# Linear expert layer: shares transposed and bias products formed inside their own batch, in PSUM banks of their own, the bias added once per two token tiles, and the next batch's chain started earlier

## The chip, the cores and the metric

One Trainium2 chip, one core. The metric is device time in microseconds (us) of one execution of the whole program. The program computes two layers of a small model, in four phases that run one after the other, each in a block of its own. The change is in the last phase only.

## The reference, cut to what matters

The last phase computes this, on 8 batches of 512 tokens with 256 channels, all in 32-bit floats (`x` is first normalised over its channels, and the output is added to the un-normalised `x`):

```python
scores = jnp.maximum(x @ gate_W + gate_b, 1e-4)          # 8 experts
p = jax.nn.softmax(scores, axis=-1)
_, topk_idx = jax.lax.top_k(p, 2)
topk_mask = jax.nn.one_hot(topk_idx, 8).sum(-2) > 0
w = jnp.maximum(p, 0.1)
w = w / take_along_axis(w, topk_idx, axis=-1).sum(-1, keepdims=True)
comb = jnp.where(topk_mask, w, 0)                         # the shares
y = jnp.einsum('bsd,edf->bsef', x, expert_W) + expert_b
out = jnp.einsum('bsef,bse->bsf', y, comb) / 2
```

Every token goes through all 8 experts, and the shares weigh the 8 results. The bias part is `comb @ expert_b`, a product with only 8 rows to sum over, and needs the shares transposed.

## The kernel before, in words

`moe_linear_phase` (from L1312) is written out by hand for five engine queues that meet only in semaphores. A batch is 512 tokens, in four token tiles `k` of 128. Experts are taken in pairs `e`; a unit `u` from 0 to 15 is one tile with one pair (k = u // 4, e = u % 4). For each unit TensorE (L1656) makes six matmuls of 128x512 into one of four banks of `o_ps`: 32-bit precision is built from an upper and a lower part of activations and weights. Odd units are weighted and taken out by ScalarE (`weigh_odd`, L1468) and summed by GpSimd (`add_odd`, L1403); even units are weighted and added into `x` by VectorE (`accumulate`, two instructions at L1570). At a tile's last unit GpSimd adds the odd sum to `x` (L1407). Unit u must wait on TensorE until the unit four earlier has been taken out of its bank.

Beside the units, each batch has a chain for the next one. It starts with the mean and variance on VectorE (`variance`, L1014 and L1019), a root on ScalarE (`root`, L1425 and L1427), the rest of the normalisation on VectorE (`normalise`, five small instructions L1024 to L1028 and four of 128x256 at L1030, which make `xn`), eight transposes on TensorE (`turn_rows`, L1612) and two copies on ScalarE (`take_rows`, L1436 and L1437). GpSimd forms the lower part (`low`, L1385), TensorE the gate product (`gate`, 16 small matmuls, L1620), VectorE the scores and the top two (`scores`, `first_choice`, `second_choice`, `shares`, L1519 to L1553), with an exponential on ScalarE (`exponents`, L1442). Then come the transposes of the shares on TensorE (`turn_comb`, L1627), a copy on ScalarE (`take_comb`, L1449), and the bias product (`biases`, L1634), which VectorE adds to two tiles of `x` in one instruction (L1564).

The order on each queue is fixed by the unit numbers. In batch n before the change:

- TensorE: bias product before units 0 and 8; `turn_rows(n+1)` after unit 3, `gate(n+1)` after 6, `turn_comb(n+1)` after 14. The gate product, the row transposes and the share transposes all use `f_ps`.
- VectorE: bias added ahead of units 0 and 8; `normalise(n+1)` after unit 0, `scores(n+1)` after 6, `first_choice` after 8, `second_choice` after 10, `shares` after 12, `variance(n+2)` after 14.
- ScalarE: `take_rows(n+1)` after unit 3, `exponents(n+1)` after 7, `take_comb(n+1)` after 14, `root(n+2)` after 15.
- GpSimd: `low(n+1)` after unit 7, and at start-up the lower weight parts of pairs 2 and 3 (L1393) only after the first batch's shares.
- SyncE stores a batch once its four tiles are done and loads the one three further on.

Before the first unit, TensorE does `turn_rows(0)`, `gate(0)`, `turn_comb(0)`, and then waits for the copied shares.

Of the kernel before, what the change touches and what calls it, by code (L numbers as in the profile page):

```python
# [7 lines left out]
ALU = mybir.AluOpType  # L8
# [5 lines left out]
P = 128  # L14
# [1297 lines left out]
def moe_linear_phase(nc, sem, A, layer, x_in, x_out):  # L1312
# [5 lines left out]
    with ExitStack() as ctx:  # L1318
# [22 lines left out]
        b_ps = ctx.enter_context(nc.psum_tensor("m1_b_ps", [P, 2, 2 * D], F32))  # L1341
# [8 lines left out]
        with nc.Block() as block:  # L1350
# [26 lines left out]
            def _(pool):  # L1377
# [10 lines left out]
                for e in range(PAIRS):  # L1388
                    if e == 2:
                        low(0)  # L1390
                        pool.wait_ge(S["comb_ready"], 1)
                    pool.wait_ge(S["w_hi"], e + 1)
                    pool.tensor_tensor(w_lo[:, e, :, :], raw[:, e, :, :], w_hi[:, e, :, :], ALU.subtract).then_inc(S["w_ready"], 1)  # L1393

                def add_odd(n, u):
# [8 lines left out]
                    if e == PAIRS - 1:  # L1404
                        pool.wait_ge(S["odd_added"], q + 1)
                        pool.wait_ge(S["acc_done"], UNITS // 2 * n + 2 * (k + 1))
                        pool.tensor_tensor(x[:, n % XB, k, :], x[:, n % XB, k, :], odd[:, k, :], ALU.add).then_inc(S["tile_done"], 1)  # L1407

                for n in range(NB):
                    for u in range(UNITS):  # L1410
                        if u % 2:
                            add_odd(n, u)
                        if u == 7 and n + 1 < NB:
                            low(n + 1)

            @block.scalar
            def _(act):
# [26 lines left out]
                def take_comb(n):  # L1444

                    act.wait_ge(S["combT_ps"], n + 1)
                    if n > 1:
                        act.wait_ge(S["b_ready"], 2 * (n - 1))
                    act.activation(combT[:, n % 2, :], f_ps[0:E, 0, :], ACT.Copy).then_inc(S["combT_ready"], 1)  # L1449
# [22 lines left out]
                upper(0)  # L1472
                upper(1)
# [3 lines left out]
                upper(2)  # L1477
                upper(3)
                take_comb(0)
                for n in range(NB):  # L1480
                    act.wait_ge(S["comb_ready"], n + 1)
                    for u in range(UNITS):
                        if u % 2:
                            weigh_odd(n, u)
                        if n + 1 < NB:
                            if u == 3:
                                take_rows(n + 1)
                            if u == 7:
                                exponents(n + 1)
                            if u == 14:  # L1490
                                take_comb(n + 1)
                        if u == 15 and n + 2 < NB:
                            root(n + 2)

            @block.vector
            def _(dve):
# [59 lines left out]
                def accumulate(n, u):  # L1556
# [5 lines left out]
                    if u % PAIRS == 0 and k % 2 == 0:  # L1562
                        dve.wait_ge(S["b_ready"], 2 * n + k // 2 + 1)
                        dve.tensor_tensor(x[:, n % XB, k:k + 2, :], b_ps[:, k // 2, :].rearrange("p (a c) -> p a c", a=2), x[:, n % XB, k:k + 2, :],  # L1564
                                          ALU.add).then_inc(S["b_added"], 1)
                        dve.wait_ge(S["b_added"], 2 * n + k // 2 + 1)
                    else:
                        dve.wait_ge(S["acc_done"], q)
# [7 lines left out]

                variance(0)
                normalise(0)
                variance(1)
                scores(0)  # L1580
# [3 lines left out]
                for n in range(NB):  # L1584
                    dve.wait_ge(S["comb_ready"], n + 1)
                    for u in range(0, UNITS, 2):
                        accumulate(n, u)
                        if n + 1 < NB:
                            if u == 0:
                                normalise(n + 1)  # L1590
                            if u == 6:
                                scores(n + 1)
                            if u == 8:
                                first_choice(n + 1)
                            if u == 10:
                                second_choice(n + 1)
                            if u == 12:
                                shares(n + 1)
                        if u == 14 and n + 2 < NB:
                            variance(n + 2)  # L1600

            @block.tensor
            def _(pe):
                pe.wait_ge(S["const_in"], 80)

                def turn_rows(n):

                    pe.wait_ge(S["xn_ready"], n + 1)
                    wait(pe, S["combT_ready"], n)
# [13 lines left out]
                def turn_comb(n):  # L1623

                    pe.wait_ge(S["comb_ready"], n + 1)
                    for k in range(4):
                        last = pe.transpose(f_ps[0:E, 0, k * P:(k + 1) * P], comb[:, n % 2, k, :], ident[:, :])  # L1627
                    last.then_inc(S["combT_ps"], 1)

                def biases(n, k):  # L1630

                    wait(pe, S["b_added"], 2 * n + k // 2 - 1)
                    for a in range(2):
                        last = pe.matmul(b_ps[:, k // 2, a * D:(a + 1) * D], combT[:, n % 2, (k + a) * P:(k + a + 1) * P], eb[:, :], start=True, stop=True)  # L1634
# [4 lines left out]
                turn_comb(0)  # L1639
                for n in range(NB):  # L1640
                    pe.wait_ge(S["xT_lo_ready"], n + 1)
                    pe.wait_ge(S["combT_ready"], n + 1)
                    for u in range(UNITS):
                        k, e = u // PAIRS, u % PAIRS
                        tok = slice(k * P, (k + 1) * P)
                        if u % PAIRS == 0 and k % 2 == 0:
                            biases(n, k)
# [10 lines left out]
                        if n + 1 < NB:  # L1658
                            if u == 3:
                                turn_rows(n + 1)  # L1660
                            if u == 6:
                                gate(n + 1)
                            if u == 14:
                                turn_comb(n + 1)
# [475 lines left out]
```

## Time and profile before

| | us |
|---|---|
| median of 3 runs | 2230.68 (2228.68 to 2231.84) |
| the profiled execution's own time | 2226.19 |
| its span, first to last instruction | 2224.4 |
| the last phase in that span, from about 1951.8 to the end | about 272.6 |

The other three phases fill the first 1951 us and their instructions are not touched. In the views, times are us from the start of the span. A timeline row is start, duration, engine, line, operation, output and inputs, shapes and how many instructions are merged; brackets at its end hold the engine's idle time before it and what ended that. "x2" with a duration of 1.60 is two instructions from the start of the first to the end of the second. PE is TensorE's matmuls, PEld its weight loads, DVE VectorE, ACT ScalarE, POOL GpSimd, SPq the queue of SyncE. Matmuls are pipelined, so that spacing between starts, not duration, is what one costs.

### The profile page before, as it was taken

What the parts mean: (1) busy time and instruction counts of PE and PEld (TensorE: products, weight loads), DVE (VectorE), ACT (ScalarE), POOL (GpSimd) and SP (SyncE); (2) the same over time, 40 slices, a digit from 0 to 9 for tenths busy, and PEclk for the clock granted to TensorE, in tenths of its full rate; (3) what the DMA queues carried; (4) which work ended last, traced back from release to release, by engine and by line L of the source; (5) the groups of instructions that cost most, each with busy time, mean ns of one, the idle gap of its engine ahead of it and who ended that gap; (6) DMA issues with size and microseconds to landing.
All of it is one profiled execution on the core that took longest, in us unless ns stands there. A gap on an engine that the chain in (4) does not pass through costs nothing. (4 is left out here: it accounts for less than half of the span.)

```text
span 2224.4 us, 32244 instructions
## 1 busy us (share of the span) xinstructions
PE 1909.3 (86%) x9910; PEld 1116.9 (50%) x9910; DVE 1656.6 (74%) x2326; ACT 1241.3 (56%) x2642; POOL 1427.7 (64%) x1164
## 2 busy tenths in 40 slices
PE   2499999999973999975799999999999998759998
PEld 1244444444422899972345454545454433347776
DVE  4477788787744646530799999999999999836664
ACT  1066666676662433325787777777778675323332
POOL 7334444543334344430899999999999999834444
PEclk9599999999875999987999999999999999969999
DMA  3554545544234454430413131222213130021100
GB/s 80 108 103 96 110 107 116 113 99 122 69 123 149 84 88 76 75 51 19 162 42 130 58 114 75 97 91 81 106 66 121 42 132 30 0 78 39 38 26 22
DMA packets 231224, 185.68 MB, mean 83 GB/s; under 512 B 148729, under 2 KB 201601, under 8 KB 231058
## 3 DMA queue, kind: packets, MB, share of 16 engines
q1 hardware_dynamic: 216178, 162.61, 25.9%
q0 software_dynamic: 13296, 17.77, 4.6%
q10 hardware_dynamic: 1584, 3.24, 0.5%
q8 instruction: 85, 1.39, 0.3%
q14 instruction: 81, 0.66, 0.1%
HBM read 134.07 MB, written 49.49 MB: 83 GB/s over the span
## 5 line engine op out<-in xcount | busy, mean ns | idle before, releaser
L1817 POOL TENSOR_TENSOR mb_dbu<-mb_dtu,mb_bbc 128x1024 f32<-128x1024 f32 x256 | 598.6, 2360 | 5.2 <-DVE mb_da_ps L1974 2.4
L473 ACT ACTIVATE ex_plain<-at_t_ps 128x512 f32<-128x512 f32 x512 | 289.5, 595 | 178.9 <-PE at_t_ps L851 176.8
L1974 DVE TENSOR_TENSOR_SCAN mb_da_ps<-mb_da_ps,mb_dbu 128x1024 f32<-128x1024 f32 x160 | 365.3, 2283 | 4.0 <-ACT mb_da_ps L1867 3.3
L2009 PE MATMUL mb_y_ps<-mb_hc,lw_ident 128*128 128x512 f32 x640 | 311.7, 610 | 43.1 <-DVE mb_hc L1981 42.7
L610 DVE TENSOR_REDUCE at_mx<-at_s_ps 128x2 f32<-128x1024 f32 x256 | 310.9, 1219 | 47.7 <-PE at_s_ps L860 46.2
L860 PE MATMUL at_s_ps<-ex_w 48*128 48x512 f32 x512 | 226.4, 504 | 37.4 <-DVE at_mx L610 24.2
L851 PE MATMUL at_t_ps<-ex_w 64*128 64x512 f32 x512 | 220.0, 487 | 11.6 <-ACT ex_plain L473 6.4
L1823 POOL TENSOR_TENSOR mb_hp<-mb_hp,mb_cbc 128x1024 f32<-128x1024 f32 x96 | 226.1, 2356 | 0.0
L1201 POOL DMA_INDIRECT x<-m_o,m_xs x71 | 113.7, 1602 | 173.3 <-DMA x<-m_o,m_xs 106.6
L1972 DVE TENSOR_TENSOR_SCAN mb_hp<-mb_da_ps,mb_dbu 128x1024 f32<-128x1024 f32 x96 | 218.9, 2280 | 6.4 <-POOL mb_dbu L1817 5.4
L2009 PEld LDWEIGHTS mb_y_ps<-mb_hc,lw_ident 128*128 128x128 f32 x640 | 118.2, 192 | 201.8 <-issue 126.5
L1981 DVE TENSOR_TENSOR mb_hc<-mb_da_ps,mb_cbc 128x1024 f32<-128x1024 f32 x160 | 195.4, 1221 | 12.6
L2009 PE MATMUL mb_y_ps<-mb_hp,lw_ident 128*128 128x512 f32 x384 | 184.2, 602 | 14.7 <-POOL mb_hp L1823 14.7
L851 PEld LDWEIGHTS at_t_ps<-ex_w 64*128 64x128 f32 x512 | 86.9, 194 | 173.3 <-ACT ex_plain L473 132.6
L1866 ACT ACTIVATE mb_da_ps<-mb_dt,lw_a_neg 128x512 f32<-128x512 f32 x256 | 172.6, 674 | 0.0
L1867 ACT ACTIVATE mb_da_ps<-mb_dt,lw_a_neg 128x511 f32<-128x511 f32 x256 | 171.9, 671 | 0.0
L1865 ACT ACTIVATE mb_da_ps<-mb_zero 128x1 f32<-128x1 f32 x256 | 43.0, 168 | 215.9 <-DVE mb_hc L1981 174.2
L1290 PE MATMUL m_y_ps<-ex_w,m_xsT_hi 128*128 x568 | 157.2, 337 | 0.1
L1403 POOL TENSOR_TENSOR m_odd<-m_odd,m_odd_in 128x256 f32<-128x256 f32 x96 | 70.6, 735 | 123.8 <-ACT m_odd_in L1468 118.6
L871 PE MATMUL at_o_ps<-ex_plain 128*32 128x512 f32 x1024 | 146.0, 644 | 0.1
L422 POOL CAST at_qk_hi<-at_qk 128x512 fp32r<-128x512 f32 x32 | 19.6, 612 | 179.8 <-DVE at_qk L754 179.8
L2009 PEld LDWEIGHTS mb_y_ps<-mb_hp,lw_ident 128*128 128x128 f32 x384 | 73.0, 192 | 104.6 <-issue 75.8
(322 smaller groups left out, 4117.8 us busy)
## 6 DMA issues: line engine op xcount, KB each, us to landing
mb_bbc<-mb_scr SPq DMA_DIRECT2D x64, 512.0 KB, 6.0
mb_cbc<-mb_scr SPq DMA_DIRECT2D x64, 512.0 KB, 5.7
ex_w<-at_scr SPq DMA_DIRECT2D x384, 64.0 KB, 2.3
m_xs<-rt_rows SPq DMA_DIRECT2D x71, 129.0 KB, 2.1
at_scr<-at_qk_hi SPq DMA_DIRECT2D x32, 256.0 KB
at_scr<-at_qk_lo SPq DMA_DIRECT2D x32, 256.0 KB
at_xin<-in_x SPq DMA_DIRECT2D x32, 128.0 KB, 2.3
ex_plain<-in_x SPq DMA_DIRECT2D x8, 512.0 KB
```

Of the source, the lines that this page charges most:

```text
L473: act.activation(probs[:, c, h, :], t_ps[:, k % 2, :], ACT.Exp, scale=SCALE).then_inc(exp_done, 1)
L610: dve.tensor_reduce(out, s_ps[:, m % 2, :, :], AX.X, ALU.max).then_inc(max_done, 1)
L851: pe.matmul(t_ps[:, k % 2, :], of_head(kst, r, h, 64, c), of_head(qst, r, h, 64), start=True, stop=True).then_inc(t_ready, 1)
L860: last = pe.matmul(s_ps[:, m % 2, a, :], of_head(qst, u % 4, h + 2 * a, 48, c), of_head(kst, u % 4, h + 2 * a, 48), start=True, stop=True)
L1817: pool.tensor_tensor(dbu[:, q % 3, :, :], dtu_2, bbc[:, 2 * p:2 * p + 2, :], ALU.mult).then_inc(S["dbu_ready"], 1)
L1823: pool.tensor_tensor(hp[:, r, :, :], hp[:, r, :, :], cbc[:, 2 * p:2 * p + 2, :], ALU.mult).then_inc(S["hp_ready"], 1)
L1866: act.activation(da_ps[:, q % 2, 0, :], dt[:, d % 2, :], ACT.Exp, scale=a_neg[:, d, 2 * p:2 * p + 1])
L1867: act.activation(da_ps[:, q % 2, 1, 1:T], dt[:, d % 2, 1:T], ACT.Exp, scale=a_neg[:, d, 2 * p + 1:2 * p + 2]).then_inc(S["da_ready"], 1)
L1972: dve.tensor_tensor_scan(hp[:, t % 3, :, :].rearrange("p j t -> p (j t)"), da, add, 0.0, ALU.mult, ALU.add).then_inc(S["scan_done"], 1)
L1974: dve.tensor_tensor_scan(da, da, add, 0.0, ALU.mult, ALU.add).then_inc(S["scan_done"], 1)
L1981: dve.tensor_tensor(hc[:, t % 2, :, :], da_ps[:, r, :, :], cbc[:, 2 * p:2 * p + 2, :], ALU.mult).then_inc(S["hc_ready"], 1)
L2009: last = pe.matmul(y_ps[:, v % 2, :], ident[:, :], src[:, j, :], start=False, stop=(q == tile_last[v] and j == 1))
```

## The change

The shares of a batch are now transposed, copied and multiplied with the biases inside that batch. They get a bank of their own (`c_ps`); the bias product has one bank where it had two, and is added after units 6 and 14 (by `add_biases`), no longer ahead of units 0 and 8. GpSimd's additions at the end of a tile become `finish`, two in a row after units 7 and 15, behind a wait for the added bias. The chain moves up. On TensorE `turn_rows(n+1)` follows unit 0, and `turn_comb(n)` with `gate(n+1)` follows unit 3. On VectorE `scores` follows unit 4, the choices units 6 and 8, `shares` and `variance(n+2)` unit 10, and `normalise(n+2)` comes after unit 14 of batch n. At start-up TensorE goes from `gate(0)` straight to the units, ScalarE splits all four weight pairs ahead of `take_rows(0)`, VectorE normalises batch 1 ahead of `scores(0)`, and GpSimd drops its wait for the shares.

```diff
-        b_ps = ctx.enter_context(nc.psum_tensor("m1_b_ps", [P, 2, 2 * D], F32))
+        b_ps = ctx.enter_context(nc.psum_tensor("m1_b_ps", [P, 2 * D], F32))
+        c_ps = ctx.enter_context(nc.psum_tensor("m1_c_ps", [P, T], F32))
@@ gpsimd
                     if e == 2:
                         low(0)
-                        pool.wait_ge(S["comb_ready"], 1)
...
-                    if e == PAIRS - 1:
-                        pool.wait_ge(S["odd_added"], q + 1)
-                        pool.wait_ge(S["acc_done"], UNITS // 2 * n + 2 * (k + 1))
-                        pool.tensor_tensor(x[:, n % XB, k, :], x[:, n % XB, k, :], odd[:, k, :], ALU.add).then_inc(S["tile_done"], 1)
+                def finish(n, k):
+                    pool.wait_ge(S["odd_added"], 4 * (PAIRS - 1) * n + (PAIRS - 1) * (k + 1))
+                    pool.wait_ge(S["b_added"], 2 * n + k // 2 + 1)
+                    pool.tensor_tensor(x[:, n % XB, k, :], x[:, n % XB, k, :], odd[:, k, :], ALU.add).then_inc(S["tile_done"], 1)
                 for n in range(NB):
-                    for u in range(UNITS):
-                        if u % 2:
-                            add_odd(n, u)
-                        if u == 7 and n + 1 < NB:
+                    for u in range(1, UNITS, 2):
+                        add_odd(n, u)
+                        if u == 5 and n + 1 < NB:
                             low(n + 1)
+                        if u in (7, 15):
+                            finish(n, u // PAIRS - 1)
+                            finish(n, u // PAIRS)
@@ scalar
                 root(0)
-                upper(0)
-                upper(1)
+                for e in range(PAIRS):
+                    upper(e)
                 take_rows(0)
                 root(1)
                 exponents(0)
-                upper(2)
-                upper(3)
-                take_comb(0)
                 for n in range(NB):
-                    act.wait_ge(S["comb_ready"], n + 1)
                     for u in range(UNITS):
+                        if u == 1:
+                            act.wait_ge(S["comb_ready"], n + 1)
                         if u % 2:
                             weigh_odd(n, u)
+                        if u == 3:
+                            take_comb(n)
                         if n + 1 < NB:
-                            if u == 3:
+                            if u == 0:
                                 take_rows(n + 1)
-                            if u == 7:
+                            if u == 5:
                                 exponents(n + 1)
-                            if u == 14:
-                                take_comb(n + 1)
-                        if u == 15 and n + 2 < NB:
+                        if u == 11 and n + 2 < NB:
                             root(n + 2)
@@ vector
-                    if u % PAIRS == 0 and k % 2 == 0:
-                        dve.wait_ge(S["b_ready"], 2 * n + k // 2 + 1)
-                        dve.tensor_tensor(x[:, n % XB, k:k + 2, :], b_ps[:, k // 2, :]..., ALU.add).then_inc(S["b_added"], 1)
-                        dve.wait_ge(S["b_added"], 2 * n + k // 2 + 1)
-                    else:
-                        dve.wait_ge(S["acc_done"], q)
+                    wait(dve, S["acc_done"], q)
...
+                def add_biases(n, k):
+                    dve.wait_ge(S["b_ready"], 2 * n + k // 2 + 1)
+                    dve.wait_ge(S["acc_done"], UNITS // 2 * n + 2 * (k + 2))
+                    rows = x[:, n % XB, k:k + 2, :]
+                    dve.tensor_tensor(rows, b_ps[:, :].rearrange("p (a c) -> p a c", a=2), rows, ALU.add).then_inc(S["b_added"], 1)
                 variance(1)
+                normalise(1)
                 scores(0)
...
                         accumulate(n, u)
+                        if u in (6, 14):
+                            add_biases(n, u // PAIRS - 1)
                         if n + 1 < NB:
-                            if u == 0:
-                                normalise(n + 1)
+                            if u == 4:
+                                scores(n + 1)
                             if u == 6:
-                                scores(n + 1)
+                                first_choice(n + 1)
                             if u == 8:
-                                first_choice(n + 1)
+                                second_choice(n + 1)
                             if u == 10:
-                                second_choice(n + 1)
-                            if u == 12:
                                 shares(n + 1)
-                        if u == 14 and n + 2 < NB:
-                            variance(n + 2)
+                        if n + 2 < NB:
+                            if u == 10:
+                                variance(n + 2)
+                            if u == 14:
+                                normalise(n + 2)
@@ tensor
                 def turn_rows(n):
                     pe.wait_ge(S["xn_ready"], n + 1)
-                    wait(pe, S["combT_ready"], n)
+                    wait(pe, S["z_ready"], n)
...
                 def biases(n, k):
-                    wait(pe, S["b_added"], 2 * n + k // 2 - 1)
+                    pe.wait_ge(S["combT_ready"], n + 1)
+                    wait(pe, S["b_added"], 2 * n + k // 2)
...
                 gate(0)
-                turn_comb(0)
                 for n in range(NB):
                     pe.wait_ge(S["xT_lo_ready"], n + 1)
-                    pe.wait_ge(S["combT_ready"], n + 1)
                     for u in range(UNITS):
-                        if u % PAIRS == 0 and k % 2 == 0:
-                            biases(n, k)
...
-                        if n + 1 < NB:
-                            if u == 3:
-                                turn_rows(n + 1)
-                            if u == 6:
+                        if u == 0 and n + 1 < NB:
+                            turn_rows(n + 1)
+                        if u == 3:
+                            turn_comb(n)
+                            if n + 1 < NB:
                                 gate(n + 1)
-                            if u == 14:
-                                turn_comb(n + 1)
+                        if u in (5, 12):
+                            biases(n, 0 if u == 5 else 2)
```

## Rows read from the trace of the kernel before

**Rows 1.** Busy time by stretch: the columns, and one stretch of 30 us.

```profile
core 0: us, PE busy (x) PEld busy (x) DVE busy (x) ACT busy (x) POOL busy (x), PEclk, DMA share, GB/s
2050.00:2080.00 30.00, 28.21 (x135) 22.04 (x134) 19.12 (x60) 9.74 (x22) 14.14 (x17) 1.00 0.12 36
```

**Rows 2.** Waits, last phase: who waited for whom, total us, times, longest.

```profile
PE m_f_ps L1612 <- DVE m_xn L1030: 18.7, 7, 15.8
PE m_f_ps L1627 <- DVE m_comb L1553: 15.4, 8, 5.7
```

**Rows 3.** Chain that ended last, one batch: start, us, engine, tile and line.

```profile
2051.47 1.09 PE m_f_ps L1612 x8
2052.56 4.14 PE m_o_ps L1656 x18
2056.70 1.68 PE m_f_ps L1620 x16
2059.89 1.05 PE m_b_ps L1634 x4
...
2072.07 0.60 PE m_f_ps L1627 x4
...
2081.31 1.09 PE m_f_ps L1612 x8
```

**Rows 4.** TensorE's timeline: last matmuls before its two halts in one batch.

```profile
2050.59 0.40 PE L1656 MATMUL m_o_ps<-m_w_lo,m_xT_hi 128*128 128x512 f32 x1
...
2070.37 0.40 PE L1656 MATMUL m_o_ps<-m_w_lo,m_xT_hi 128*128 128x512 f32 x1
```

**Rows 5.** VectorE's timeline around a batch's start, bias to `xn`.

```profile
2046.96 0.69 DVE L1564 TENSOR_TENSOR m_x<-m_b_ps,m_x 128x512 f32<-128x512 f32 x1 [2.04 <-PE m_o_ps L1656]
2047.69 1.00 DVE L1570 SCALAR_TENSOR_TENSOR m_x<-m_o_ps,m_comb,m_x 128x256 f32<-128x256 f32 x2
2048.61 0.15 DVE L1024 TENSOR_TENSOR m_rs<-m_rs 128x4 f32<-128x4 f32 x1
...
2049.40 0.60 DVE L1028 TENSOR_TENSOR m_rs<-m_rs 128x4 f32<-128x4 f32 x1
2050.04 1.38 DVE L1030 TENSOR_SCALAR m_xn<-m_x,m_mv,m_rs 128x256 f32<-128x256 f32 x4
```

**Rows 6.** GpSimd's timeline around the same batch's start.

```profile
2044.81 1.60 POOL L1403 TENSOR_TENSOR m_odd<-m_odd,m_odd_in 128x256 f32<-128x256 f32 x2 [3.58 <-ACT m_odd_in L1468]
2046.49 0.73 POOL L1407 TENSOR_TENSOR m_x<-m_x,m_odd 128x256 f32<-128x256 f32 x1
2049.24 0.74 POOL L1403 TENSOR_TENSOR m_odd<-m_odd,m_odd_in 128x256 f32<-128x256 f32 x1 [2.02 <-ACT m_odd_in L1468]
```

**Rows 7.** Timeline at start-up: GpSimd beside VectorE's four `xn` instructions.

```profile
1960.47 4.69 POOL L1393 TENSOR_TENSOR m_w_lo<-m_raw,m_w_hi 128x1024 fp32r<-128x1024 f32 x2 [8.61 <-ACT m_w_hi L1454]
1960.48 5.48 DVE L1030 TENSOR_SCALAR m_xn<-m_x,m_mv,m_rs 128x256 f32<-128x256 f32 x4
```

**Rows 8.** Timeline of the start-up, from the first gate product on.

```profile
1970.08 3.58 PE L1620 MATMUL m_f_ps<-m_gw,m_xT 128*128 128x8 f32 x16 [2.03 <-ACT m_xT_hi L1437]
1970.17 2.35 POOL L1385 TENSOR_TENSOR m_xT_lo<-m_xT,m_xT_hi 128x1024 fp32r<-128x1024 f32 x1 [5.01 <-ACT m_xT_hi L1437]
1970.24 0.20 ACT L1427 ACTIVATE m_rs<-m_rs 128x4 f32<-128x4 f32 x1
1979.31 1.02 PE L1627 MATMUL m_f_ps<-m_ident,m_comb 128*8 128x128 f32 x4 [5.65 <-DVE m_comb L1553]
1983.07 0.80 PE L1656 MATMUL m_o_ps<-m_w_hi,m_xT_hi 128*128 128x512 f32 x1
...
2014.34 1.13 PE L1634 MATMUL m_b_ps<-m_eb,m_combT 8*128 8x256 f32 x4
```

**Rows 9.** Busy time by stretch at start-up, columns as in the first group.

```profile
1986.00:1989.00 3.00, 3.00 (x8) 2.32 (x8) 2.67 (x9) 0.35 (x1) 0.00 (x0) 0.50 0.00 0
1989.00:1992.00 3.00, 3.00 (x16) 2.45 (x16) 2.41 (x6) 0.80 (x3) 0.81 (x1) 0.97 0.00 0
```

**Rows 10.** TensorE's timeline in the third phase, after idle times of 2.36 and 3.35 us.

```profile
1881.73 1.99 PE L2009 MATMUL mb_y_ps<-mb_hc,lw_ident 128*128 128x512 f32 x4 [2.36 <-DVE mb_hc L1981]
1921.27 3.47 PE L2009 MATMUL mb_y_ps<-mb_hc,lw_ident 128*128 128x512 f32 x4 [3.35 <-DVE mb_hc L1981]
```

**Rows 11.** Timeline of the end of the span.

```profile
2217.70 0.40 PE L1656 MATMUL m_o_ps<-m_w_lo,m_xT_hi 128*128 128x512 f32 x1
...
2220.34 0.72 POOL L1407 TENSOR_TENSOR m_x<-m_x,m_odd 128x256 f32<-128x256 f32 x1
2221.09 0.37 SPq L1370 DMA_DIRECT2D x<-m_x  x1
```

More of the change, by code:

```diff
@@ L1448, in take_comb @@
                         act.wait_ge(S["b_ready"], 2 * (n - 1))
-                    act.activation(combT[:, n % 2, :], f_ps[0:E, 0, :], ACT.Copy).then_inc(S["combT_ready"], 1)
+                    act.activation(combT[:, n % 2, :], c_ps[0:E, :], ACT.Copy).then_inc(S["combT_ready"], 1)
                 def upper(e):
@@ L1561, in accumulate @@
                     dve.wait_ge(S["o_ready"], UNITS * n + u + 1)
-                    if u % PAIRS == 0 and k % 2 == 0:
-                        dve.wait_ge(S["b_ready"], 2 * n + k // 2 + 1)
-                        dve.tensor_tensor(x[:, n % XB, k:k + 2, :], b_ps[:, k // 2, :].rearrange("p (a c) -> p a c", a=2), x[:, n % XB, k:k + 2, :],
-                                          ALU.add).then_inc(S["b_added"], 1)
-                        dve.wait_ge(S["b_added"], 2 * n + k // 2 + 1)
-                    else:
-                        dve.wait_ge(S["acc_done"], q)
+                    wait(dve, S["acc_done"], q)
                     for a in range(2):
@@ L1625, in turn_comb @@
                     pe.wait_ge(S["comb_ready"], n + 1)
+                    wait(pe, S["combT_ready"], n)
                     for k in range(4):
-                        last = pe.transpose(f_ps[0:E, 0, k * P:(k + 1) * P], comb[:, n % 2, k, :], ident[:, :])
+                        last = pe.transpose(c_ps[0:E, k * P:(k + 1) * P], comb[:, n % 2, k, :], ident[:, :])
                     last.then_inc(S["combT_ps"], 1)
                 def biases(n, k):
-                    wait(pe, S["b_added"], 2 * n + k // 2 - 1)
+                    pe.wait_ge(S["combT_ready"], n + 1)
+                    wait(pe, S["b_added"], 2 * n + k // 2)
                     for a in range(2):
-                        last = pe.matmul(b_ps[:, k // 2, a * D:(a + 1) * D], combT[:, n % 2, (k + a) * P:(k + a + 1) * P], eb[:, :], start=True, stop=True)
+                        last = pe.matmul(b_ps[:, a * D:(a + 1) * D], combT[:, n % 2, (k + a) * P:(k + a + 1) * P], eb[:, :], start=True, stop=True)
                     last.then_inc(S["b_ready"], 1)
```

## The prediction

> **What bounds the kernel now.** I read four views, in this order. The busy time by stretch [rows 1] says that the last phase is TensorE's: 28.21 of 30 us busy at full clock, VectorE 19.12, GpSimd 14.14, ScalarE 9.74. So only what makes TensorE wait or work can move the end. The waits [rows 2] name the two halts: the row transposes wait for `xn`, the share transposes for `comb`. The chain [rows 3] gives the period: from one batch's row transposes at 2051.47 to the next at 2081.31 is 29.84 us, and nearly every piece is TensorE's. Last, TensorE's timeline [rows 4] gives the size of the halts. Eighteen matmuls take 4.14 us [rows 3], so 0.23 each and a unit of six 1.37. The last matmul before the row transposes starts at 2050.59, so these could have begun at 2050.82; they began at 2051.47, a halt of 0.65. Likewise 2070.37 + 0.23 = 2070.60 against 2072.07, a halt of 1.47. The period adds up: 96 matmuls 21.9, row transposes 0.9, gate 1.8, two bias products 2.5, share transposes 0.5, halts 2.1. All that a better order can win per batch is the 2.1, and at the start-up the 5.65 us that TensorE is idle for the first shares [rows 8].
>
> **The share halt goes.** `turn_comb(n)` follows unit 3 of its own batch, long after the shares. Its copy by ScalarE (0.6 us) has units 4 and 5 (2.7 us) to hide under before the bias product. I cost these moves at 0, and the work itself stays: same transposes, products and additions, so 27.6 us per batch without halts (0.1 less than before, as gate and share transposes are adjacent). If the cover were gone, the bias product would wait 0.6.
>
> **The row halt grows: the main term.** `turn_rows(n+1)` now follows unit 0, while VectorE makes its `xn` only after unit 14 of the batch before and after a bias addition. Between the two TensorE has units 15 and 0 alone, 2.74 us. VectorE needs, from the rows of the same instructions [rows 5]: 0.2 until it sees unit 14 (as before its bias addition at 2046.96; unit 0 ended at about 2046.8), 1.03 for the two accumulations, 0.6 for the bias addition, 5 x 0.2 for the small instructions (2048.61 to 2049.40 is four of them), 1.38 for L1030, 0.05 to TensorE. That is 4.26, so the halt is at least 4.26 - 2.74 = 1.5 us however free the rest is.
>
> To that comes GpSimd. The fifth small instruction takes 0.60 us where its like takes 0.15, and it ends (2050.00) just as a GpSimd addition (2049.24 + 0.74) ends [rows 5, 6]. At start-up four `xn` instructions take 5.48 us instead of 1.38; beside them lie two GpSimd instructions of 4.69 in all [rows 7]. The first instruction ended with the first of these, the second with the second, and the last two were free. So a running GpSimd instruction holds such a VectorE instruction to its end, and one gets through per GpSimd instruction. The accumulations and the bias addition, which read PSUM, show no such loss [rows 5].
>
> The Trainium skill's page "SBUF — State Buffer", section "Who interferes with whom", speaks against the change here: it tells of a lock on a shared port pair, taken for a whole instruction, by every tensor-tensor operation with both inputs in SBUF and by tensor-scalar operations. By that rule all nine instructions can be held; if only L1028 and L1030 could, where rows show it, the halt below would be 2.8 and the sum 3.6 less. Up to those two lines the trace agrees.
>
> Where do the two meet? GpSimd's last two additions of the batch start 0.74 us after unit 15 (2044.81 against 2044.07, 0.23 after its last matmul started) and span 1.60, then 0.08 and 0.73 for the tile's end [rows 6]. The change puts a second tile's end behind that: busy from +0.74 to about +3.9. VectorE's small instructions begin at +0.46. Two pass; the third (L1026, of the same operation and shape as the fifth) is held to +1.5, the fifth to +2.4, the first `xn` instruction to +3.2, the second to +4.1; the last two take 0.66. TensorE starts the transposes at +4.8 instead of +1.37: a halt of 3.4. Bounds: 1.5 (no holding) to 4.0 (VectorE also late into unit 14). I take 3.4, as its rows are the same engines and lines. VectorE's stretch from unit 6 on (bias, both choices, shares, variance, four accumulations) comes out at 24.95 after the row transposes, against 25.0 for the end of unit 14: just in time, with no slack; hence the upper bound. `root(n+2)` after unit 11 keeps ScalarE waiting for the variance, and unit 13's weighing behind it, by 0.9 us; its bank is needed two units later, so 0.
>
> From the start of batch 1 to the end of the last unit is 2014.24 to 2217.93 = 203.7 before [rows 8, 11]. After: six batches with a halt, 6 x (27.6 + 3.4) = 186.0, and a last one without row transposes and gate, 24.9: 210.9. **+7.2.**
>
> **Start-up.** The units can follow the gate at 1973.8 instead of 1983.07 [rows 8]. Unit 0 ends at 1976.4, at the lower clock (0.43 us a matmul). Then `turn_rows(1)` waits for the second `xn` and for `z_ready`, that is `scores(0)`, queued behind `normalise(1)`. That starts at 1970.5 [rows 8] and meets three GpSimd instructions without a gap, since the wait for the shares is gone: `low(0)` to 1972.5 and two weight parts of 2.35 to 1977.2. Held once by each, it ends at about 1979.0, the scores at 1979.8. Row transposes 1.8, units 1 to 3 at the lower clock 7.7, share transposes and gate 2.6: unit 4 starts at 1991.9. Then 12 units 16.5 and two bias products 2.5: batch 1 starts at 2010.9 against 2014.24. **-3.3** (from 0, if the raised clock comes later, to -6, if it comes sooner; before, it came at 1989.2, after 6 us of units [rows 8, 9]). Splitting all weights before `take_rows(0)` hides under ScalarE's idle time up to 1968.1: 0, or +2 if weight data landed late.
>
> **End.** Both tiles' ends now stand behind the last unit, one more instruction of 0.72 before the store [rows 11]: **+0.7**. The bias addition ends earlier than GpSimd's odd sums, so its wait is free.
>
> **Clock.** TensorE now pauses 3.4 us in each of six batches, with only transposes behind it. In the third phase a pause of 3.35 was followed by four matmuls in 3.47 us, one of 2.36 by four in 1.99 [rows 10]: the granted clock, 2.4 GHz before, was at its lower level, 1.2 GHz, after the one and not after the other. A longer pause is thus more likely than not to cost about 1.6 (3.47 against 1.88 to 1.99). I take 4.5 times in six, midway between half and all: **+7.2**, with 0 and 6 x 2 = 12 as ends.
>
> **Sum.** 7.2 - 3.3 + 0.7 + 7.2 = +11.8. The profiled execution took 2226.19 (span 2224.4 plus 1.8 around it), 4.5 below the median of the runs shown; the difference is put on the median: 2230.7 + 11.8 = 2242.5.
>
> **The rivals.**
> 1. The halt is as I say, but the clock holds: +4.6, 2235.3. For it: TensorE's halts of 1.3 us left the clock at 1.00 [rows 1]. Against: [rows 10].
> 2. Faster: GpSimd and VectorE hardly meet, because ScalarE or GpSimd is out of step there. The halt is 1.5, short enough for the clock: 6 x (27.6 + 1.5) + 24.9 = 199.5, so -4.2 - 3.3 + 0.7 = -6.8, 2223.9. It decides below a halt of 2.6, with the clock held, where 6 x 2.6 is the 15.8 that the rest wins (rival 4). Against: GpSimd's four additions follow unit 15 by semaphores, and cannot be earlier or later by much.
> 3. VectorE becomes the bound from unit 6 on and starts its bias addition some 1.5 us late: halt 5 us, 6 x 1.6 more and the clock lost every time (+2.4): 2254. For it: the walk above leaves that stretch no slack. Against: 1.5 us is as much as all the holding that I counted at the batch's start.
> 4. The change does what it says in full, no halt is left: 6 x 27.6 + 24.9 = 190.5, with start-up and end -15.8, 2214.9. Against: the 1.5 us above needs no contention.
>
> **Chances.** Forecast 0.51, rival 1 0.2, rival 2 0.14, rival 3 0.11, rival 4 0.04. A measurement of this kernel tells about 0.2% (4.5 us) from no change. Rival 2 and 4 are faster, less a part of rival 2 near the line: 0.15. Rival 1 straddles the upper line: with half of it and the rest of rival 2 the same has 0.15. Slower 0.70. The range leaves out rival 4 and the outer parts of rivals 2 and 3: 2226 to 2252.
>
> **What would show it.** Right: the waits list has one large TensorE entry, row transposes for L1030, six times 3 us or more, none for `comb`; L1030 and the small instructions before it stretch beside GpSimd's; the period is 31 to 33 us; the clock by stretch falls below 1.00 in units 1 to 3. Wrong: L1030 at 1.38 for four and a period below 29.8, or the first unit not at about 1974. The weakest steps are how many pauses cost the clock, and where exactly GpSimd's additions fall.

## The result, and the profile after

The changed kernel is slower: median 2249.57 us of 6 runs (2243.15 to 2252.72) against 2229.94 of 6 runs of the kernel before; ratio 1.0089, 95% interval 1.0073 to 1.0105, some 19.6 us. The forecast was 2242.5 in a range of 2226 to 2252. The profiled execution took 2250.02, its span 2248.2. Its last phase, from the ScalarE table load at its head to the span's end, takes 291.98 us (from 1956.22) against 272.64 before (from 1951.76). That is 19.3 more, so all of the difference lies there.

Busy time of the whole span, after:

```profile
PE 1930.6 (86%) x9910; PEld 1131.0 (50%) x9910; DVE 1673.1 (74%) x2326; ACT 1240.6 (55%) x2642; POOL 1426.2 (63%) x1164
```

TensorE has the same 9910 matmuls and is busy some 21 us longer (1909.3 before). Waits (columns as in [rows 2]), and the chain of one batch (as in [rows 3]):

```profile
PE m_f_ps L1619 <- DVE m_xn L1030: 37.9, 7, 15.9
PE m_f_ps L1619 <- DVE m_p L1524: 3.5, 1, 3.5
```

```profile
2119.04 1.97 PE m_f_ps L1619 x8
2121.01 5.87 PE m_o_ps L1661 x18
2127.32 1.69 PE m_f_ps L1627 x16
2131.87 1.05 PE m_b_ps L1643 x4
...
2153.17 1.97 PE m_f_ps L1619 x8
```

The wait for `comb` is gone. The wait for `xn` went from 18.7 [rows 2] to 37.9, and without the first wait of 15.9 it is six of 3.67. The period is 34.13 where it was 29.84. Two pieces have grown though their instructions are the same: the eight row transposes, 1.97 where [rows 3] has 1.09, and the eighteen matmuls behind them, 5.87 where it has 4.14. That is the clock, as the busy time by stretch says (columns as in [rows 1]):

```profile
2110.00:2140.00 30.00, 26.34 (x117) 21.20 (x116) 16.86 (x46) 8.78 (x20) 12.14 (x15) 0.89 0.10 36
2119.00:2122.00 3.00, 2.96 (x11) 2.76 (x12) 0.86 (x2) 0.95 (x2) 0.00 (x0) 0.50 0.41 137
2122.00:2125.00 3.00, 3.00 (x9) 2.30 (x8) 0.00 (x0) 1.82 (x4) 0.43 (x1) 0.56 0.46 160
```

Here is the stretch that ends the pause:

```profile
2117.00:2119.50 2.50, 0.46 (x2) 0.46 (x3) 2.43 (x7) 0.00 (x0) 0.55 (x1) 0.66 0.39 137
```

Right behind the pause (2119 to 2122) the granted clock is 0.50, the lower of the two levels, 1.2 GHz, and the units of the next 5 us or so still run at it. Read in stretches of half a microsecond, the clock falls at about 2117.8, in the pause itself, and is back at about 2124.6: it is low for 6.8 us, 5.6 of them behind the start of the row transposes. The pauses before 2050.65, 2084.85, 2153.17 and 2187.30 look the same. The first one differs: the clock falls only at 2018.8, 1.25 us behind the start of the transposes at 2017.55, and is back at 2022.2, low for 3.4 us.

VectorE and GpSimd at the same halt; the columns are start, us, engine and line, and idle time before in brackets:

```profile
2112.10 2.08 DVE L1566 SCALAR_TENSOR_TENSOR m_x<-m_o_ps,m_comb,m_x 128x256 f32<-128x256 f32 x4
2114.29 0.69 DVE L1578 TENSOR_TENSOR m_x<-m_b_ps,m_x 128x512 f32<-128x512 f32 x1
2114.89 0.45 DVE L1024 TENSOR_TENSOR m_rs<-m_rs 128x4 f32<-128x4 f32 x1
2115.38 0.17 DVE L1025 TENSOR_SCALAR m_rs<-m_mv 128x4 f32<-128x4 f32 x1
2115.58 0.63 DVE L1026 TENSOR_TENSOR m_rs<-m_rs 128x4 f32<-128x4 f32 x1
2116.25 0.65 DVE L1027 TENSOR_SCALAR m_rs<-m_rs 128x4 f32<-128x4 f32 x1
2116.93 0.64 DVE L1028 TENSOR_TENSOR m_rs<-m_rs 128x4 f32<-128x4 f32 x1
2117.61 1.38 DVE L1030 TENSOR_SCALAR m_xn<-m_x,m_mv,m_rs 128x256 f32<-128x256 f32 x4
```

```profile
2113.56 0.74 POOL L1403 TENSOR_TENSOR m_odd<-m_odd,m_odd_in 128x256 f32<-128x256 f32 x1 [4.13 <-ACT m_odd_in L1472]
2114.59 1.60 POOL L1403 TENSOR_TENSOR m_odd<-m_odd,m_odd_in 128x256 f32<-128x256 f32 x2 [0.29 <-ACT m_odd_in L1472]
2116.15 1.40 POOL L1409 TENSOR_TENSOR m_x<-m_x,m_odd 128x256 f32<-128x256 f32 x2
2114.98 0.40 PE L1661 MATMUL m_o_ps<-m_w_lo,m_xT_hi 128*128 128x512 f32 x1
2119.04 1.97 PE L1619 MATMUL m_f_ps<-m_ident,m_xn 128*128 128x128 f32 x8 [3.66 <-DVE m_xn L1030]
```

GpSimd's five additions lie nearly without a gap from 2113.56 to 2117.55. Beside them four of VectorE's small instructions, which take 0.15 to 0.2 each when they are free, take 0.45, 0.63, 0.65 and 0.64; each ends just as a GpSimd addition ends. The last matmul of unit 0 starts at 2114.98, and by the 0.23 of the prediction the halt is 2119.04 - 2115.21 = 3.83. It is 3.82 to 3.83 in all six batches (the profile's own idle time reads 3.66 to 3.67).

### The profile page after: what moved, and what is told of

Read it like the earlier page. It is cut to its first block and busy times, and to the rows that moved or that the text cites. A ratio compares the mean times of both kernels' runs of the same rounds, so it can differ in the third digit from the quotient of the medians.

```text
span 2248.2 us, 32281 instructions
## 1 busy us (share of the span) xinstructions
PE 1930.6 (86%) x9910; PEld 1131.0 (50%) x9910; DVE 1673.1 (74%) x2326; ACT 1240.6 (55%) x2642; POOL 1426.2 (63%) x1164
## 5 line engine op out<-in xcount | busy, mean ns | idle before, releaser
L2015 PE MATMUL mb_y_ps<-mb_hc,lw_ident 128*128 128x512 f32 x640 | 316.3, 618 | 41.4 <-DVE mb_hc L1987 40.8
L422 POOL CAST at_qk_hi<-at_qk 128x512 fp32r<-128x512 f32 x32 | 19.5, 609 | 181.2 <-DVE at_qk L754 181.2
L1566 DVE SCALAR_TENSOR_TENSOR m_x<-m_o_ps,m_comb,m_x 128x256 f32<-128x256 f32 x128 | 61.7, 482 | 96.7 <-PE m_o_ps L1661 93.1
```

Of the source, the lines that this page charges most:

```text
L2015: last = pe.matmul(y_ps[:, v % 2, :], ident[:, :], src[:, j, :], start=False, stop=(q == tile_last[v] and j == 1))
```

## The experiments

All are edits of the changed kernel, whose line numbers they keep to within a few. What stands in the halt is in dispute (VectorE's fixed order alone, or GpSimd beside it), and so is what the pause costs through the clock. One table for all; "idle" is TensorE's idle time ahead of the row transposes, from batch 1 on; "low clock" is how many of those six pauses cost the clock; "period" is from one batch's transposes to the next's; these three and the last phase are read from the one profiled execution of each kernel; the kernel before ran beside them, median 2228.42 for the first four (31 runs) and 2228.56 for the last four (9 runs).

| kernel | median us (runs) | ratio to before, 95% | last phase | idle | low clock | period |
|---|---|---|---|---|---|---|
| after | 2249.57 (6) | 1.0089 (1.0073 to 1.0105) | 291.98 | 3.67 | 6 of 6 | 33.1, then 34.1 to 34.2 |
| e1_fill | 2234.84 (10) | 1.0029 (1.0017 to 1.0042) | 277.75 | 0.98 | 0 of 6 | 31.57 |
| e2_late_finish | 2228.08 (10) | 0.9999 (0.9987 to 1.0011) | 275.91 | 2.71 | 2 of 6 | 30.56; 33.44, 32.22 |
| e3_rows_late | 2223.45 (10) | 0.9987 (0.9973 to 1.0001) | 263.42 | 1.53 | 0 of 6 | 29.39 |
| e4_old_chain | 2220.23 (10) | 0.9966 (0.9952 to 0.998) | 263.83 | 1.08 | 0 of 6 | 28.95 |
| e5_bias_behind | 2208.6 (5) | 0.9912 (0.9899 to 0.9926) | 253.11 | 0 | 0 of 6 | 27.65 |
| e6_after_bias_behind | 2227.6 (1) | | 272.03 | 2.01 | 3 of 6 | 29.85; 31.47 |
| e7_all | 2205.89 (5) | 0.9902 (0.9889 to 0.9916) | 251.28 | 0 | 0 of 6 | 27.65, once 28.15 |
| e8_root_first | 2237.02 (1) | | 285.1 | 3.67 | 5 of 6 | 31.53, then 33.1 to 34.1 |

**Is it the pause that costs the clock?** The first kernel leaves VectorE's halt as it is, and fills it.

```diff
                 def turn_rows(n):
 
+                    if n > 1:
+                        pe.wait_ge(S["combT_ready"], n - 1)
+                        for _ in range(12):
+                            pe.matmul(c_ps[:, :], xT_hi[:, (n - 1) % 2, 0, 0:P], w_hi[:, 0, 0, :], start=True, stop=True)
                     pe.wait_ge(S["xn_ready"], n + 1)
```

> The changed kernel, with 12 extra matmuls of 128x512 (2.7 us at the full clock, result unused) put on TensorE ahead of the row transposes' wait, in batches 1 to 6, into the bank of the transposed shares. They fit into the halt of 3.8 us. Clock theory (the pause makes the clock fall, and that costs 1.6 to 2.6 us a batch beside the pause itself): the first transpose of a batch starts no later, the clock stays at 1.00, some 12 to 15 us off 2249.6: about 2236, still slower than before. Rival (the low clock after the halt has another cause, or costs nothing that the next halt would not take anyway): 2248 to 2251.

TensorE's timeline and one stretch of busy time:

```profile
2105.71 2.91 PE L1618 MATMUL m_c_ps<-m_w_hi,m_xT_hi 128*128 128x512 f32 x12
2109.59 1.09 PE L1623 MATMUL m_f_ps<-m_ident,m_xn 128*128 128x128 f32 x8 [0.98 <-DVE m_xn L1030]
```

```profile
2109.60:2112.60 3.00, 3.00 (x17) 2.62 (x18) 0.81 (x2) 1.87 (x3) 0.00 (x0) 1.00 0.49 132
```

The row transposes start 3.88 us behind unit 0, as late as after the change, and yet the clock is 1.00, they take 1.09, and the period is 31.57 against 34.13: 2.6 us a batch, for more work. The phase is 14.2 shorter and the median 14.7, of which up to 1.5 may lie between the two sets of runs: the kernel before had 2229.94 beside the changed kernel and 2228.42 here. The kernel is still 0.3% slower than the one before, as expected. So the pause costs twice, once as idle time and once in the clock. From the row transposes behind the first of the six pauses to the end of the last unit it takes 209.2 us (2014.87 to 2224.03), against 223.65 of the changed kernel (2017.55 to 2241.20): the clock is 14.5 us of the loss.

**Is GpSimd in the halt?** The two `finish` of a batch's last tiles go behind unit 1 of the next batch, away from VectorE's small instructions; VectorE's order stays.

```diff
-                        if u in (7, 15):
+                        if u == 1 and n:
+                            finish(n - 1, 2)
+                            finish(n - 1, 3)
+                        if u == 7 or u == 15 and n == NB - 1:
                             finish(n, u // PAIRS - 1)
```

> The changed kernel, with GpSimd's two tile ends behind unit 15 moved behind unit 1 of the next batch; TensorE's and VectorE's orders are untouched. Holding theory (a running GpSimd instruction holds a VectorE instruction to its end): L1027 and L1028 take 0.17 and not 0.65, so the halt shrinks by 0.9 to 1.0 from 3.8 to 2.9, 6 us in six batches; if the shorter pause saves some of the clock, up to 14 more: 2230 to 2244, 2242 if not. Rival (VectorE is late by its own load, GpSimd does not matter): halt 3.8, 2248 to 2251.

VectorE, GpSimd and TensorE at one halt:

```profile
2072.46 0.63 DVE L1026 TENSOR_TENSOR m_rs<-m_rs 128x4 f32<-128x4 f32 x1
2073.12 0.17 DVE L1027 TENSOR_SCALAR m_rs<-m_rs 128x4 f32<-128x4 f32 x1
2073.32 0.16 DVE L1028 TENSOR_TENSOR m_rs<-m_rs 128x4 f32<-128x4 f32 x1
2071.46 1.60 POOL L1403 TENSOR_TENSOR m_odd<-m_odd,m_odd_in 128x256 f32<-128x256 f32 x2 [0.27 <-ACT m_odd_in L1475]
2074.96 1.09 PE L1622 MATMUL m_f_ps<-m_ident,m_xn 128*128 128x128 f32 x8 [2.72 <-DVE m_xn L1030]
```

L1026 is held to the end of the odd additions, as before the edit. L1027 and L1028, whose neighbours were the two `finish`, fall from 0.65 and 0.64 to 0.17 and 0.16: 0.96 together, and the halt is 0.96 shorter. The period is 30.56 where the clock holds, which four pauses of six did. Six halts shorter by 0.96 are 5.8. The clock costs 2.9 and 1.7 in two pauses, 4.5 in all, where the changed kernel lost 14.5, so 10.0 more: together 15.8. The phase is 16.1 shorter. The ratio, 0.9999, can't be told from the kernel before. The median, 2228.08, is 2 below the expected 2230 to 2244, as most of the clock was kept.

**Does the place of the row transposes decide?** They go behind unit 2, with `take_rows` and `gate` as much later.

```diff
-                            if u == 0:
+                            if u == 1:
                                 take_rows(n + 1)
...
-                        if u == 0 and n + 1 < NB:
+                        if u == 2 and n + 1 < NB:
                             turn_rows(n + 1)
                         if u == 3:
                             turn_comb(n)
-                            if n + 1 < NB:
-                                gate(n + 1)
+                        if u == 4 and n + 1 < NB:
+                            gate(n + 1)
```

> The changed kernel, with the row transposes on TensorE behind unit 2 instead of unit 0 (the two copies on ScalarE behind unit 1's weighing, the gate product behind unit 4). VectorE's and GpSimd's orders are untouched. Theory (the halt is the gap between xn and the place where TensorE asks for it): two units of 1.37 more cover, halt 3.8 - 2.7 = 1.1, clock kept, 16 + 14 us off: about 2219, 11 faster than before. Rival (VectorE is the bound from unit 6 on and is late everywhere): TensorE waits elsewhere for the same time and the kernel stays above 2240.

The halt is 1.69 (idle 1.53) and not the 1.1 that two units of cover leave of 3.83. VectorE and GpSimd:

```profile
2072.92 1.93 DVE L1030 TENSOR_SCALAR m_xn<-m_x,m_mv,m_rs 128x256 f32<-128x256 f32 x4
2073.00 0.72 POOL L1403 TENSOR_TENSOR m_odd<-m_odd,m_odd_in 128x256 f32<-128x256 f32 x1
```

Units 1 and 2 now run ahead of the transposes, so unit 1's odd addition comes earlier and meets L1030: four in 1.93, not 1.38. The 0.55 is what was missing. Edits of TensorE's order move GpSimd's additions too. With no low clock left, the phase is 28.6 shorter. The median, 2223.45, misses the expected 2219, and its ratio, 0.9987 with an interval up to 1.0001, does not tell it from the kernel before. The rival (above 2240) is out.

**The shares moved alone.** Shares and bias as in the change, the rest of the chain where it was before.

```diff
-                            if u == 0:
+                            if u == 3:
                                 take_rows(n + 1)
...
+                            if u == 0:
+                                normalise(n + 1)
...
-                            if u == 14:
-                                normalise(n + 2)
...
-                        if u == 0 and n + 1 < NB:
-                            turn_rows(n + 1)
                         if u == 3:
                             turn_comb(n)
                             if n + 1 < NB:
-                                gate(n + 1)
+                                turn_rows(n + 1)
+                        if u == 6 and n + 1 < NB:
+                            gate(n + 1)
```

> One part alone: shares transposed and bias product formed in their own batch, own banks, bias added after units 6 and 14, units starting right after the first gate product, as in the changed kernel; but the chain for the next batch at its places of before (xn after unit 0, row transposes after unit 3, gate after 6, scores after 6, choices after 8 and 10, shares after 12, variance after 14). Theory (the moved chain alone made it slower): the share halts (7 x 1.5) and the 5.6 us at the start go, row halts stay near 0.7: 2213 to 2219, some 14 faster than before. Rival (the new order of bias and shares costs something itself): 2228 or more.

This half of the change is worth having: 0.9966, and the period falls from 29.82 to 28.95. That is less than the share halt of 1.47, since the row halt grew from 0.65 to about 1.2. The median, 2220.23, is 8 us below the kernel before and not the expected 14: the first row transposes also waited 3.96 us, with the clock low for 6.8 us around them. The rows of one later halt:

```profile
2076.80 0.74 DVE L1027 TENSOR_SCALAR m_rs<-m_rs 128x4 f32<-128x4 f32 x1
...
2077.77 1.83 DVE L1030 TENSOR_SCALAR m_xn<-m_x,m_mv,m_rs 128x256 f32<-128x256 f32 x4
...
2079.66 1.09 PE L1617 MATMUL m_f_ps<-m_ident,m_xn 128*128 128x128 f32 x8 [1.08 <-DVE m_xn L1030]
```

Again two GpSimd additions are met, one by L1027 and one by L1030.

**The bias addition out of the way.** On the third kernel's order, the batch's second bias addition goes behind `normalise(n+2)`. So `xn` no longer waits for it, and `finish`, which does wait for it, can't start beside the small instructions.

```diff
-                        if u in (6, 14):
+                        if u == 6 or u == 14 and n + 2 >= NB:
                             add_biases(n, u // PAIRS - 1)
...
                                 normalise(n + 2)
+                                add_biases(n, 2)
```

> As the kernel with the row transposes behind unit 2, and VectorE adds the second bias product behind the normalisation instead of ahead of it (batches 0 to 5). Theory (what stands on VectorE between unit 14 and xn, and what GpSimd does at that time, sets the halt): the bias addition's 0.6 leaves the path, and GpSimd's two tile ends, which wait for it, come later and hold nothing ahead of xn (0.9): the row halt falls from 1.7 to 0.2, period from 29.4 to 27.9, about 9 us off: 2214. Rival (VectorE's load from unit 6 on is the bound, order within it does not matter): halt 1.7, 2223.

```profile
2063.55 1.75 DVE L1030 TENSOR_SCALAR m_xn<-m_x,m_mv,m_rs 128x256 f32<-128x256 f32 x4
2065.21 0.68 DVE L1578 TENSOR_TENSOR m_x<-m_b_ps,m_x 128x512 f32<-128x512 f32 x1
2066.04 1.42 POOL L1409 TENSOR_TENSOR m_x<-m_x,m_odd 128x256 f32<-128x256 f32 x2 [1.87 <-DVE m_x L1578]
2065.69 0.40 PE L1662 MATMUL m_o_ps<-m_w_lo,m_xT_hi 128*128 128x512 f32 x1
2065.93 0.82 PE L1620 MATMUL m_f_ps<-m_ident,m_xn 128*128 128x128 f32 x6
```

`xn` is done at 2065.30, TensorE wants it at 2065.92, and no halt is left. The period, 27.65, is the 27.6 of work that the prediction counted. The ratio to the kernel before is 0.9912, and the median, 2208.6, is some 5 below what was expected (2214).

The same swap alone, on the changed kernel:

> The changed kernel with that one swap alone (second bias addition behind the normalisation), row transposes still behind unit 0. Theory: halt 3.8 - 0.6 - 0.9 = 2.3 in each of six batches, and the lower clock after it in few of them (pauses of 2.9 us: two in six): phase of 292 us shortened to about 270. Rival (load): halt 3.8, lower clock in all six.

TensorE at two of the halts:

```profile
2074.68 1.09 PE L1620 MATMUL m_f_ps<-m_ident,m_xn 128*128 128x128 f32 x8 [2.01 <-DVE m_xn L1030]
2104.54 1.69 PE L1620 MATMUL m_f_ps<-m_ident,m_xn 128*128 128x128 f32 x8 [2.01 <-DVE m_xn L1030]
```

VectorE at the first of these two halts:

```profile
2071.41 0.22 DVE L1024 TENSOR_TENSOR m_rs<-m_rs 128x4 f32<-128x4 f32 x1
2072.06 0.60 DVE L1027 TENSOR_SCALAR m_rs<-m_rs 128x4 f32<-128x4 f32 x1
2072.89 1.73 DVE L1030 TENSOR_SCALAR m_xn<-m_x,m_mv,m_rs 128x256 f32<-128x256 f32 x4
```

The halt falls from 3.83 to 2.16. The rows split the 1.67. From the end of unit 14 to the first small instruction it is 0.78 less (the addition and the gap before it). The five small instructions, up to L1030, take 1.48 and not 2.72, as only L1027 is held for long. L1030 gives 0.35 back: four in 1.73 and not 1.38. The two `finish` no longer run beside these instructions, but the last two odd additions do, and they now hold L1027 and the first `xn` instruction. Pauses of equal length go both ways: the transposes take 1.09 after one and 1.69 after the next, and the periods alternate between 31.47 and 29.85. Each of the three losses is a low clock of 3.4 us and costs 1.6.

**Start-up.** `root(1)` goes ahead of `take_rows(0)`, so that `normalise(1)` can run before GpSimd's three long instructions (2.35, then two in 4.67).

```diff
-                take_rows(0)
                 root(1)
+                take_rows(0)
```

> The changed kernel with root(1) ahead of take_rows(0) at start-up and nothing else. Theory (the first row halt of 3.9 us comes from three GpSimd instructions, 7 us in all, that hold three of VectorE's small ones): these run ahead of GpSimd, the first row halt falls to 0.5 or less, batch 1 starts 2 to 3.5 us earlier, less if the clock rises later; the six later halts stay at 3.8. Rival: that halt is the wait for the scores whatever GpSimd does, 3.9 again.

```profile
1967.99 3.42 DVE L1030 TENSOR_SCALAR m_xn<-m_x,m_mv,m_rs 128x256 f32<-128x256 f32 x4
1968.86 2.39 POOL L1386 TENSOR_TENSOR m_xT_lo<-m_xT,m_xT_hi 128x1024 fp32r<-128x1024 f32 x1 [5.18 <-ACT m_xT_hi L1441]
1971.22 4.73 POOL L1393 TENSOR_TENSOR m_w_lo<-m_raw,m_w_hi 128x1024 fp32r<-128x1024 f32 x2
1972.61 1.06 DVE L1522 TENSOR_SCALAR m_p<-m_p 128x32 f32<-128x32 f32 x1
1973.92 2.07 DVE L1524 TENSOR_TENSOR m_p<-m_p,m_small 128x32 f32<-128x32 f32 x1
```

Batch 1's first unit comes 52.34 us into the phase, not 56.13, and the first halt is 1.43 instead of 3.86; the expected 0.5 or less is missed. The long instructions catch an `xn` instruction (four in 3.42) and then two of the scores. What is held changed, that something is held did not.

**All together**: the fifth kernel, with `root(1)` first, `variance(n+2)` after unit 4 and `root(n+2)` after unit 5.

> Row transposes behind unit 2, second bias addition behind the normalisation, variance(n+2) moved to behind unit 4 and its root to behind unit 5, and at start-up root(1) ahead of take_rows(0). Theory: unit 14 is met on time (0.4 off the halt, so none is left), unit 13's weighing no longer waits for the root, and at the start the second normalisation runs ahead of GpSimd's three long instructions, some 2 us off: period 27.7, 2210 to 2213. Rival (the x of batch n+2 is not yet loaded at unit 4, VectorE waits for it and passes that on): later than the kernel without these moves, 2216 or more.

```profile
2038.00:2065.00 27.00, 27.00 (x131) 21.57 (x130) 19.39 (x59) 9.11 (x21) 13.89 (x17) 1.00 0.12 40
```

TensorE is busy for all 27 of 27 us. VectorE is no longer late for unit 14: its accumulation at 2060.49 has waited 1.40 us for TensorE. The median, 2205.89, is the best here and below the expected 2210, but with 5 runs each it can't be told from the fifth kernel's 2208.6 (ratios 0.9902 and 0.9912, intervals overlapping).

## Why the prediction was right, and which terms were off

**The share halt** went, at no cost, as forecast: no wait for `comb` is left, and 27.65 us of work per batch is the 27.6 counted.

**The row halt**: forecast 3.4, measured 3.83, within the bounds of 1.5 to 4.0. Its parts can be read from the rows. VectorE's order alone was put at 1.5. Held time was put at 1.9; the four stretched instructions come to 2.37, and four free ones of 0.16 would be 0.64, so it is 1.7. The rest is the last accumulation: unit 14 ended at 2112.47, VectorE could have begun at 2112.67, and began the third and fourth instruction of that group at 2113.18, so 0.5 late. 1.5 + 1.7 + 0.5 = 3.7; the last 0.1 is the gap between the accumulation's end at 2114.18 and the bias addition at 2114.29. The prediction gave VectorE's stretch "no slack" and then took the lateness at nothing. That was the step that made the halt too short, by 0.43 a batch or 2.6 in six. It is rival 3's mechanism at a third of its size. What held VectorE back so long was not tested by itself. Two things in the traces are each large enough. Between 2102.55 and 2109.48 five small instructions of the choices and the shares take 0.44 to 0.66 beside GpSimd's additions, where their like take 0.18 to 0.19 without one, 2.0 us more in all. And the variance stands in that stretch with 1.8 us; in the last kernel, which has it after unit 4, unit 14 is met in time.

Which instructions are held was only half right: two small ones and two `xn` were forecast, four small ones and no `xn` came. L1024 was already held, as the late accumulation and the bias put it beside GpSimd's running additions. The Trainium skill's "SBUF — State Buffer", section "Who interferes with whom", says that a VectorE instruction with two inputs in SBUF contends with a GpSimd instruction that reads SBUF, and that a tensor-scalar one can, where its operands meet further conditions. The trace agrees in all four, L1027 among them, a tensor-scalar instruction of four elements per partition (0.17 free, 0.65 held). L1025, which fell between two additions here (0.17), is held at start-up (2.29), and L1030 is held there [rows 7] and in the third kernel. So "all nine can be held" is borne out, and the forecast with L1028 and L1030 alone (halt 2.8) is not.

**The clock** was the term that was mis-sized: +7.2 forecast, 14.5 measured against the first kernel (of the periods, 1.5 over its 31.57 for the first pause and 2.6 for each of the next four). Both factors were low. The clock fell after six pauses of six, not 4.5. And a loss mostly cost 2.6, not 1.6. The prediction took its price from one pause of the third phase [rows 10], and for that pause it was right: the clock was low from about 1920.9 to 1924.3, and the next matmuls ran at the full clock:

```profile
1924.58 1.88 PE L2009 MATMUL mb_y_ps<-mb_hp,lw_ident 128*128 128x512 f32 x4
```

What failed was to carry that one price over to all pauses. In all the kernels here a loss in the row pauses is a low clock of either 3.4 or 6.8 us. The short ones cost 1.5 to 1.7 (the first pause of the changed kernel, 1.5), the long ones 2.4 to 2.9; five of the six here were long. Why a pause gets a long one is open. With 14.5 in its place the forecast would have been 2249.8.

**From batch 1 to the last unit** the trace has 2012.35 to 2241.20 = 228.85 against 203.7: +25.15, forecast 7.2 + 7.2 = 14.4. The 10.7 too little is 7.3 of the clock, 2.6 of the halt, and 0.8 over, of which no row stands out (0.05 a batch is work, 27.65 for 27.6).

**Start-up**: forecast -3.3, measured 56.13 - 62.48 = -6.35, just outside its bounds (0 to -6). TensorE's timeline of the changed kernel:

```profile
1984.42 1.73 PE L1619 MATMUL m_f_ps<-m_ident,m_xn 128*128 128x128 f32 x8 [3.47 <-DVE m_p L1524]
...
1987.66 0.59 PE L1661 MATMUL m_o_ps<-m_w_hi,m_xT_lo 128*128 128x512 f32 x1
1988.09 0.40 PE L1661 MATMUL m_o_ps<-m_w_lo,m_xT_hi 128*128 128x512 f32 x1
```

The clock was raised from about 1981.3, in the halt, fell at about 1984.7, just behind the start of the row transposes, and was back at about 1988.1, in unit 1. The forecast took all of units 1 to 3 at the lower level (7.7 us); they took 5.3. The way there was right: the scores, held behind `normalise(1)`, keep TensorE waiting (L1524), and L1024, L1025 and L1026, held once by each long GpSimd instruction, take 1.99, 2.29 and 2.27. This error had the other sign and hid 3.05 of the first. That was luck, and the range hangs on it: with the start-up as forecast the changed kernel would have come out at about 2252.6, just above 2252.

**End**: +0.7 forecast, measured 7.00 (2241.20 to 2248.2) against 6.47, +0.5.

Together: 25.15 - 6.35 + 0.53 = 19.3, where the forecast had 14.4 - 3.3 + 0.7 = 11.8. The size of the change, +19.6, is thus two thirds more than the forecast +11.8; its way and its main mechanism, a row halt with a lower clock behind it, are the forecast's. **The rivals**: rival 1 (clock holds) fell with the first kernel, which shows both what the clock takes and that the changed kernel lost it. Rival 2 (hardly any meeting, halt 1.5) fell with the second. Rival 3 came partly true: VectorE 0.5 late, and the clock lost every time. Rival 4 (no halt, 2214.9) is what the fifth kernel reaches, by another order than the change's; its last phase is 19.5 shorter than before, where rival 4 has 15.8, nearly all of it at start-up: batch 1 begins at 55.24 into the phase, 7.2 earlier than before, and the forecast had 3.3.

## What to carry to other kernels

A chain that is moved up saves nothing unless the time between the last instruction that it must wait for and the one that needs it is counted on every engine in its fixed order; here one bias addition of 0.69 put behind `xn`, and the transposes two units later, turned +0.9% into -0.9%. Small VectorE instructions on that path are cheap only when no GpSimd addition runs beside them: 0.16 each free, 0.64 held. And a TensorE pause is to be priced twice, the idle time and the low clock behind it, until the clock is back; where it can't be removed, matmuls whose result nobody reads can fill it.

## What the runs showed of the hardware

- In a row of GpSimd additions without gaps, one held VectorE instruction gets through per addition, whatever its size among those seen: tensor-tensor 128x4 (0.16 to 0.63), tensor-scalar 128x4 (0.17 to 0.65), tensor-scalar 128x32 (0.18 to 1.06 beside longer ones). Bias additions and accumulations, which have an input in PSUM, took their usual 0.69 and 0.5 in the same stretch.
- Idle times of 3.67 cost the clock in 11 of 12 pauses (two kernels), of 2.71 in 2 of 6, of 2.01 in 3 of 6, of 1.53 and less in 0 of 18 (e1_fill, e3_rows_late and e4_old_chain). There is no sharp length here, and 2.01 lost it more often than 2.71; what else decides in one batch and not in the next was not settled.
- In these row pauses a loss is a low clock of about 3.4 us (six times) or about 6.8 us (ten times), with nothing between. The short ones cost 1.5 (the first of the changed kernel) to 1.7, the long ones 2.4 (e8_root_first) to 2.9 (33.44 against 30.56 in e2_late_finish).
- Twelve matmuls with no use made a kernel some 14 us faster (phase 14.2, median 14.7).
